# A mixture of experts on one core: experts of three units on rows sorted by expert on the chip

## The reference

```python
xm = _ln(x, ln2_g, ln2_b)
logits = xm @ gate_w.T + gate_b
topv, topi = jax.lax.top_k(logits, TOPK)
gates = jax.nn.softmax(topv, axis=-1)
onehot = jax.nn.one_hot(topi, NEXP, dtype=x.dtype)
comb = jnp.einsum('bnk,bnke->bne', gates, onehot)
moe_out = jnp.zeros_like(x)
for e in range(NEXP):
    he = jax.nn.gelu(xm @ exp_w1[e] + exp_b1[e], approximate=False)
    oe = he @ exp_w2[e] + exp_b2[e]
    moe_out = moe_out + comb[..., e:e + 1] * oe
return x + moe_out
```

## Time and profile before

| | |
|---|---|
| median of 3 runs | 875.37 us |
| profiled execution | 875.9 us |
| its span | 874.1 us |
| PE, DVE, ACT, POOL busy | 792.7, 534.2, 475.8, 275.1 us |
| embedding and attention | 0 to 423 us |
| mixer and dense layer | 423 to 661 us |
| chunks 12 to 95 | 661 to 874 us |

### The profile page before, as it was taken

The page is one execution under the profiler, slowest core; times in us unless marked ns, Lnnn a source line. Parts: engine busy times, 40 slices in busy tenths (PEclk is TensorE's granted clock), DMA queues, the critical chain, the costliest instruction groups (busy, mean ns, idle before and its releaser), DMA issues.

```text
span 874.1 us, 16507 instructions
## 1 busy us (share of the span) xinstructions
PE 792.7 (91%) x6000; PEld 716.2 (82%) x6000; DVE 534.2 (61%) x1404; ACT 475.8 (54%) x1292; POOL 275.1 (31%) x483
## 2 busy tenths in 40 slices
...
DMA packets 37505, 47.32 MB, mean 54 GB/s; under 512 B 4721, under 2 KB 32497, under 8 KB 37425
## 3 DMA queue, kind: packets, MB, share of 16 engines
...
...
## 4 chain that ended last, share of the span: by engine, by line
PE 37%; DVE 5%; POOL 4%; DMA 2%; ACT 2%; issue 1%; SPq 0%; ACTq 0%; DVEq 0%; POOLq 0%
PE mix_ring L1320 11%; PE mix_scores L1335 7%; PE mix_scores L1336 3%; PE mix_ring L1262 2%; PE mix_ring L1211 2%; PE mix_ring L1233 2%; PE mix_ring L1274 2%; PE mix_scores L1200 1%; PE mix_ring L1173 1%; POOL mix_bias_part L1142 1%; DMA mix_stage<-in_w 1%; PE mix_ring L1224 1%; ACT mix_probs L1377 1%; POOL mix_bias_sum L1144 1%; DMA mix_w_out<-in_w_mix_out 1%
## 5 line engine op out<-in xcount | busy, mean ns | idle before, releaser
L454 POOL TENSOR_SCALAR attn_probs<-attn_probs,attn_inverse 128x128 f32<-128x128 f32 x128 | 47.8, 374 | 288.3 <-DVE attn_inverse L744 280.5
L1570 DVE TENSOR_TENSOR mix_hid_lo<-mix_gelu,mix_hid_hi 128x512 fp32r<-128x512 f32 x96 | 80.5, 840 | 68.2 <-ACT mix_hid_hi L1430 67.4
L1335 PE MATMUL mix_scores<-mix_w,mix_hid_hi 128*128 128x384 f32 x384 | 115.9, 359 | 0.4 <-DVE mix_hid_lo L1570 0.3
L1426 ACT ACTIVATE mix_gelu<-mix_ring,mix_b 128x512 f32<-128x512 f32 x96 | 65.7, 684 | 86.4 <-PE mix_ring L1320 79.6
L1336 PE MATMUL mix_scores<-mix_w,mix_hid_lo 128*128 128x192 f32 x384 | 96.5, 251 | 0.0
L1102 POOL TENSOR_SCALAR mix_probs<-mix_probs,mix_inverse 128x128 f32<-128x128 f32 x192 | 73.5, 403 | 65.9 <-DVE mix_inverse L1528 65.9
L613 ACT ACTIVATE attn_probs<-ps_scores,attn_neg_max 128x128 f32<-128x128 f32 x128 | 45.2, 366 | 77.8 <-DVE attn_neg_max L740 77.8
L1335 PEld LDWEIGHTS mix_scores<-mix_w,mix_hid_hi 128*128 128x128 f32 x384 | 72.2, 188 | 5.8 <-DVE mix_hid_lo L1570 1.6
L1336 PEld LDWEIGHTS mix_scores<-mix_w,mix_hid_lo 128*128 128x128 f32 x384 | 73.1, 190 | 3.3
L1377 ACT ACTIVATE mix_probs<-mix_scores,mix_neg_max 128x128 f32<-128x128 f32 x192 | 67.6, 389 | 1.9 <-DVE mix_neg_max L1520 1.8
L1142 POOL TENSOR_SCALAR mix_bias_part<-mix_b,mix_gates 128x192 f32<-128x192 f32 x64 | 38.4, 614 | 94.7 <-DVE mix_gates L1606 93.6
...
## 6 DMA issues: line engine op xcount, KB each, us to landing
...
attn_v_rows<-v_rows SPq DMA_DIRECT2D x128, 96.0 KB, 3.7
...
mix_stage<-in_w SPq DMA_DIRECT2D x10, 192.0 KB, 3.2
mix_stage<-in_w SPq DMA_DIRECT2D x5, 384.0 KB, 4.3
...
h_rows<-hin SPq DMA_DIRECT2D x8, 192.0 KB, 2.0
mix_h<-h_rows SPq DMA_DIRECT2D x4, 384.0 KB, 4.9
```

The source lines that it names most:

```text
L454: last = nc.gpsimd.tensor_scalar(probs[:, n, j, :], probs[:, n, j, :], inverse[:, n, j:j + 1], float(D) ** -0.5, ALU.mult, ALU.mult)
L1335: nc.tensor.matmul(ps_out[:, b, 0:2 * D], hid_hi[:, i % 3, tile], w2[:, c, :, :], start=c == 0, stop=False)
L1426: nc.scalar.activation(gelu[:, i % 2, :], ring[:, bank("L1", i), :], ACT.Gelu, bias=b1[:, f * HC + c:f * HC + c + 1]).then_inc(chunk_read, 1)
L1570: nc.vector.tensor_tensor(hid_lo[:, i % 3, :], gelu[:, i % 2, :], raw(hid_hi[:, i % 3, :]), ALU.subtract).then_inc(lo_ready, 1)
```

## The change

Unit 0 stays as it was: 24 chunks, each expert on all rows. Of units 1 to 3 a row goes only to the two experts that its gates name. The steps are these.

- **Gates early.** The gate steps of units 1 to 3 stand at chunks 12 to 21 (of unit 0).
- **Slots.** PE counts, by matmuls with a triangle and with ones, how many rows above chose each expert (CNT); DVE makes of it each row's two slots in a DRAM tensor `sorted`, which has 1792 rows for each expert (SLOT).
- **Scatter.** POOL sends each tile's rows (192 values, four gates and the token's number, 788 bytes a row) there by indirect DMA, twice, 8 DMAs a unit. SP had filled `sorted` with zero rows by 28 DMAs, ahead of the weights of the next `load_weights`.
- **Table.** DVE makes a table of 15 groups of 256 rows: the expert of each and its place (TABLE).
- **Groups.** For each group SP reads the place to a register and loads its rows into one of 3 buffers `group_rows`; PE turns them (GX), POOL copies the first layer's weights of the expert read from the table (GW1), and three blocks of two hidden chunks run as before on 256 rows (G1, G2). DVE multiplies by the gate and adds (GF), and POOL adds the rows to the DRAM tensor `home` by two indirect DMAs (GA) at the token numbers that lie in the same buffer.
- **End.** When all groups are home, one DMA copies `home` to the output.

The core of the diff:

```diff
+    SORTED = UNITS - 1
+    GROUP_TILES = 2
+    GT = GROUP_TILES * P
+    BLOCKS_OF = SORTED * UT // GT + 1
+    SLOTS = BLOCKS_OF * GT
+    SORTS = (TWO * SORTED * UT + NEXP * (GT - 1)) // GT
+    ROW = D + NEXP + 1
+    FAR = float(2 * NEXP * SLOTS)
...
+            i = FIRST + 3 * (u - 1)
+            put(i, ("EX", (u, 0)), ("EX", (u, 1)))
             if u + 1 < UNITS:
-                for part in range(NORM_PARTS - 1):
-                    put(i + 3 + part, ("EN", (u + 1, part)))
+                put(i, *(("EN", (u + 1, part)) for part in range(2)))
+            put(i + 1, ("EG", u))
+            if u + 1 < UNITS:
+                put(i + 1, *(("EN", (u + 1, part)) for part in range(2, ROOTS)))
+            put(i + 2, ("EB", u), ("RANK", u))
+            if u + 1 < UNITS:
+                put(i + 2, ("EN", (u + 1, ROOTS)), ("B", u + 1))
+            put(i + 3, ("EXP", u), ("CNT", u), ("GATES", u), ("SLOT", u), ("SCATTER", u))
+        put(FIRST + 3 * (UNITS - 1), ("TABLE", 0))
...
+        blocks = [(g, k) for g in range(SORTS) for k in range(BLOCKS)]
+
+        def second_block(i):
+            g, k = blocks[i]
+            order.append(("G2", i))
+            if k == BLOCKS - 1:
+                order.append(("GF", g))
+                order.append(("GA", g))
+
+        order.append(("GW1", 0))
+        order.append(("GX", 0))
+        for i, (g, k) in enumerate(blocks):
+            order.append(("G1", i))
+            if k == 0 and g + 1 < SORTS:
+                order.append(("GW1", g + 1))
+            if k == 1 and g + 1 < SORTS:
+                order.append(("GX", g + 1))
+            if i >= LAG:
+                second_block(i - LAG)
...
+            def load_group(g):
+                q = sp.value_load(table[0:1, 0, g:g + 1], min_val=0, max_val=NEXP * BLOCKS_OF - 1)
+                if g >= 3:
+                    sp.wait_ge(came_home, 16 * GROUP_TILES * (g - 2))
+                sp.dma_start(group_rows[:, g % 3, :, :], dram["sorted"].rearrange("(q b p) r -> q p b r", p=P, b=GROUP_TILES)[bass.ds(q, 1), :, :, :].rearrange("q p b r -> p (q b) r")).then_inc(group_loaded[g % 3], 16)
+                e = sp.value_load(table[0:1, 1, g:g + 1], min_val=0, max_val=NEXP - 1)
+                if g >= 2:
+                    sp.wait_ge(chunk_read, CHUNKS0 + BLOCKS * (g - 1))
+                    sp.wait_ge(biased_group, g - 1)
+                sp.dma_start(group_b1[:, g % 2, :], dram["b1"][:, bass.ds(e * HC + HC, HC)]).then_inc(group_weights[g % 2], 16)
+                sp.dma_start(group_b2[:, g % 2, :], dram["b2"][:, bass.ds(e * D + D, D)].to_broadcast([P, D])).then_inc(group_weights[g % 2], 16)
...
+            sp.wait_ge(pads_ready, 4)
+            for q in range(NEXP * BLOCKS_OF):
+                sp.dma_start(dram["sorted"][q * GT:(q + 1) * GT, :].rearrange("(b p) r -> p b r", p=P), pattern).then_inc(prefilled, 16)
+            sp.dma_start(dram["home"][SORTED * UT:SORTED * UT + GT, :].rearrange("(b p) d -> p b d", p=P), pattern[:, :, 0:D]).then_inc(prefilled, 16)
             load_weights(1)
...
+            sp.wait_ge(scattered, 16 * TWO * UNIT * SORTED)
+            sp.wait_ge(table_ready, 1)
+            for g in range(SORTS):
+                load_group(g)
+                if g == 0:
+                    sp.wait_ge(expert_free, NEXP * UNIT)
+                    sp.dma_start(dram["out"][0:UT, :].rearrange("(b p) d -> p b d", p=P), total[:, :, :]).then_inc(first_stored, 16)
+            sp.wait_ge(came_home, 16 * GROUP_TILES * SORTS)
+            sp.dma_start(dram["out"][UT:TOKENS, :], dram["home"][0:SORTED * UT, :]).then_inc(out_stored, 16)
+            sp.wait_ge(first_stored, 16)
+            sp.wait_ge(out_stored, 16)
...
-                        pool.wait_ge(v_ready, TILES)
+                    pool.wait_ge(d2_filled, TILES)
...
+            def scatter(u):
+                pool.wait_ge(xn_ready, u + 1)
+                nc.gpsimd.iota(rows_of(u)[:, :, ROW - 1].bitcast(I32), pattern=[[P, UNIT]], base=(u - 1) * UT, channel_multiplier=1).then_inc(tokens_put, 1)
+                pool.wait_ge(tokens_put, u)
+                pool.wait_ge(gates_put, u)
+                pool.wait_ge(slotted, u)
+                if u == 1:
+                    pool.wait_ge(prefilled, 16 * (NEXP * BLOCKS_OF + 1))
+                for b in range(UNIT):
+                    for k in range(TWO):
+                        nc.gpsimd.indirect_dma_start(dram["sorted"], bass.IndirectOffsetOnAxis(ap=slots_at[:, u - 1, k, b:b + 1], axis=0),
+                                                     rows_of(u)[:, b, 0:ROW], None).then_inc(scattered, 16)
+
+            def put_weights(g):
+
+                if g == 0:
+                    pool.wait_ge(table_ready, 1)
+                    pool.wait_ge(weights_lo, 3 * FFNS)
+                    pool.wait_ge(d2_filled, TILES)
+                if g >= 2:
+                    pool.wait_ge(l1_filled, CHUNKS0 + BLOCKS * (g - 1))
+                e = pool.value_load(table[0:1, 1, g:g + 1], min_val=0, max_val=NEXP - 1)
+                nc.gpsimd.tensor_copy(w_dense[:, g % 2, :], raw(w_all[:, bass.ds(e, 1), 0:W1].rearrange("p e n -> p (e n)"))).then_inc(weights_put, 1)
+
+            def bring_home(g):
+                pool.wait_ge(group_free, GROUP_TILES * (g + 1))
+                if g == 0:
+                    pool.wait_ge(home_set, 16 * SORTED)
+                    pool.wait_ge(prefilled, 16 * (NEXP * BLOCKS_OF + 1))
+                else:
+                    pool.wait_ge(came_home, 16 * GROUP_TILES * g)
+                for b in range(GROUP_TILES):
+                    nc.gpsimd.indirect_dma_start(dram["home"], bass.IndirectOffsetOnAxis(ap=group_rows[:, g % 3, b, ROW - 1:ROW].bitcast(I32), axis=0),
+                                                 total[:, g % 2 * GROUP_TILES + b, :], None, compute_op=ALU.add).then_inc(came_home, 16)
...
+            def group_rows_turned(g):
+                pe.wait_ge(group_loaded[g % 3], 16 * (g // 3 + 1))
+                slot_free("GX", g)
+                to = ring[:, bank("GX", g), :]
+                for b in range(GROUP_TILES):
+                    last = turn_rows(to, group_rows[:, g % 3, b, :], slice(b * P, (b + 1) * P), slice(GT + b * P, GT + (b + 1) * P))
+                last.then_inc(gx_filled, 1)
...
+            def group_x_split(g):
+                act.wait_ge(gx_filled, g + 1)
+                if g == 0:
+                    act.wait_ge(xt_ready, 2 * UNITS)
+                    act.wait_ge(l1_filled, CHUNKS0)
+                else:
+                    act.wait_ge(gx_ready, g)
+                if g >= 2:
+                    act.wait_ge(l1_filled, CHUNKS0 + BLOCKS * (g - 1))
+                of = ring[:, bank("GX", g), :]
+                for part in range(2):
+                    last = nc.scalar.activation(xt_full[:, part, 0:GT], of[:, part * GT:(part + 1) * GT], ACT.Identity, scale=ln2[:, 0, part:part + 1], bias=ln2[:, 1, part:part + 1])
+                last.then_inc(gx_full, 1)
+                act.wait_ge(gx_full, g + 1)
+                nc.scalar.activation(group_x[0][:, :, g % 2 * GT:(g % 2 + 1) * GT], xt_full[:, :, 0:GT], ACT.Copy).then_inc(gx_hi, 1)
...
+            def group_x_low(g):
+                dve.wait_ge(gx_hi, g + 1)
+                half_of = slice(g % 2 * GT, (g % 2 + 1) * GT)
+                nc.vector.tensor_tensor(group_x[1][:, :, half_of], xt_full[:, :, 0:GT], raw(group_x[0][:, :, half_of]), ALU.subtract).then_inc(gx_ready, 1)
+                dve.wait_ge(group_loaded[g % 3], 16 * (g // 3 + 1))
+                sorts.then(nc.vector.tensor_tensor(gate_parts[:, :, :], group_rows[:, g % 3, :, D:D + NEXP], of_group[:, g:g + 1, :].to_broadcast([P, GROUP_TILES, NEXP]), ALU.mult))
+                sorts.then(nc.vector.tensor_reduce(out=group_gate[:, g % 3, :], in_=gate_parts[:, :, :], op=ALU.add, axis=X))
...
+            def group_sum(g):
+                if g < 2:
+                    dve.wait_ge(first_stored, 16)
+                else:
+                    dve.wait_ge(came_home, 16 * GROUP_TILES * (g - 1))
+                dve.wait_ge(group_weights[g % 2], 32 * (g // 2 + 1))
+                mine = lambda b: total[:, g % 2 * GROUP_TILES + b, :]
+                gate = lambda b: group_gate[:, g % 3, b:b + 1]
+                bank_of = lambda b: ps_out[:, g % 2 * GROUP_TILES + b, :]
+                for b in range(GROUP_TILES):
+                    last = nc.vector.tensor_scalar(mine(b), group_b2[:, g % 2, :], gate(b), 1.0, ALU.mult, ALU.mult)
+                last.then_inc(biased_group, 1)
+                dve.wait_ge(biased_group, g + 1)
+                for b in range(GROUP_TILES):
+                    if b < GROUP_TILES - 1:
+                        dve.wait_ge(group_done, g * (GROUP_TILES - 1) + b + 1)
+                    else:
+                        dve.wait_ge(hid_used, CHUNKS0 + BLOCKS * (g + 1))
```

(47 more changed lines are left out.)

230 lines of the change are left out of this document (175 added, 55 removed).

## The result

The changed kernel takes 968.68 us (967.05 to 970.76, 4 runs) beside 875.59 us of the kernel before in the same runs: 1.106 times as long, 95% interval 1.103 to 1.109. The forecast was 978 us, its range 925 to 1035. The profiled execution has 968.75 us for a span of 967.0.

What follows compares the result with a forecast made beforehand. The prediction took PE to bound the kernel before, and the loop of group rows to bound the changed one: front 750 + 12 x 16.0 + end 34 = 976 of span, forecast 978 us, 8-in-10 range 925 to 1035.

Steps and rivals of the forecast that it cites:

- Front: Up to the first group: table ends about 721, scatter landed 731, group 0's rows 735, its turn and split 738, group 2's turn 750.
- its cover of 13 us: Before the first group: DVE's 13 us of own work from 664 hides POOL's delayed weight copies; without it, up to 10 us.
- The loop: Group stage: with three row buffers, turn, sums of g-3, two DMAs home, load and next turn follow one another each round.
- T: Time of one round of the group loop: taken as 16.0 us, between 14.6 and 16.4; bounds 11.9 and 20.6.
- PE's work at the lower clock (16.4): Group stage: idle PE falls to 1.2 GHz, where a round's PE work takes 16.4 us, longer than the loop.
- The sum of the links alone: Group loop: turn to sums 6.4, way home 4.85, SP's wake 0.1 and load 3.2 give 14.6 us a round.
- End: After the last turn: PE's remaining blocks 17, last gelu, copies and sums, way home 4.85, final copy 7.5; sum 34 us.
- Signs: New profile: PE busy half to two thirds in the group stage, idle before turns, turns 14 to 17 us apart, clock 0.5 to 0.8.
- Rivals 1 and 2: Group loop hidden, PE-bound: 1 about 879 us, slightly slower, chance 0.05; 2, with early front, 869 or some 865, faster, 0.05.
- rival 1: Group stage: PE stays the bound, T 8.2, about 879 us, slightly slower because end and front eat PE's gain; chance 0.05.
- Rival 3: Way home: accumulating DMAs are slow, landing 7.7 and contended loads, T 20.6, 1037 us in all; chance 0.11.
- Rival 4: Before the groups: prefill DMAs in SP's queue delay the mixer's weight load; at 100 GB/s 15 us late, 993; chance some 0.08.

## Why the prediction was right, point by point

- **Front.** Right. Table at 722.8 (721 forecast), last scatter issued at 729.9 and landed 2.4 later (731), turn of group 0 at 735.7 (735), first group block at 740.4 (738), turn of group 2 at 752.6 (750). From the first turn to its block took 4.6 us, where the forecast had 3 for turn and split: this turn ran at the lower clock, 2.1 us. POOL's later bias work cost nothing that shows, as its cover of 13 us held.
- **The loop.** Right in its parts and shown by buffers, order, add and idle time, each changed alone. T is 15.13, not 16.0: this step was mis-sized by 0.87 x 12 = 10 us, a little more than the whole error of 9; the turn of group 2, 2.6 late, took part of it back. I had taken PE's work at the lower clock (16.4) as the nearer bound, and that leaning was the mistake: the clock was 0.79 and not 0.50, and PE idled 3.5 us and more in every round, so its work was never the bound. Of the loop's links the clock lengthened the turn, 2.19 in place of 1.23. The sum of the links alone, 14.6, was nearer the truth. Of the parts, the second DMA home came 1.87 after the first and not 1.25 (the add's issue is 1.55, the plain one of the earlier trace rows 0.95), and the load took 2.65, not 3.2; the landing, 3.3 to 3.6 against the 3.6 taken, was right. So the turn and the home DMAs were taken too short and the load too long, and these partly offset each other.
- **End.** 33.1 us behind the last turn against 34 (the terms as they stand add up to 33.2). That it fits is in part luck: the last sums ended 18.3 us behind the turn and not 20.8, and the copy took 6.2 and not 7.5; the way home took 5.4 and not 4.85, and the 3.2 us behind the last sums, for the pair ahead, I had not counted at all.
- **Signs.** Rounds of 14 to 17 us, the clock and the idle time before the turn came as said. PE's busy share in the group stage did not: 72% (158.6 of 220), over the two thirds.
- **Rivals 1 and 2** (PE-bound) are what the change becomes once the loop and the copy are out of the way, 8.32 us a round. Even then it is not faster, as rival 1 had it: 885.5 where 879 was worked out. Front and end take what 27 chunks less give.
- **Rival 3.** The adding DMAs are slower than plain ones, by 1.4 us a round, not by 6.
- **Rival 4.** The prefill's 28 DMAs were issued in 21.7 us and landed 8.2 us after their issue by the median, so they were through by about 462, before the next load was issued at 475.3. The mixer's stage kept its pace: PE was busy 211.8 us from 423.5 to 661.2 against 212.1 before, and that load landed 0.6 us later, at 482.0. The prefill in SP's queue:

```profile
432.25 21.72 SPq L1157 DMA_DIRECT2D sorted_rows<-mix_xt_full  x28
```
